# Query stage of a two-layer attention and expert kernel: sums of squares split between two engines, and the order of VectorE's steps

## The reference, cut to what matters

```python
x = x + _L0_xattn_ref(_layernorm(x, axis=-1), ctx_2048, ...)

# inside: 16 heads (NH) of 128 columns (HD)
q = (hidden_states @ Wq + bq).reshape(b, s, NH, HD)
var = jnp.mean(q * q, axis=-1, keepdims=True)      # one per token and head
q = q * jax.lax.rsqrt(var + 1e-6) * qn_w
```

## Time and profile before

| | us |
|---|---|
| median of 3 runs (4677.71 to 4683.45) | 4682.44 |
| the profiled execution: its own time | 4708.63 |
| the profiled execution: span of the profile | 4706.5 |
| of it the query stage | first 218 |

### The profile page before, as it was taken

How to read it: one execution, slowest core, us unless ns; L and a number is a source line. 1 busy time by engine, 2 the same in 40 slices (tenths; PEclk the granted TensorE clock), 3 DMA queues, 4 the chain that set the end, 5 groups by cost and what they waited for, 6 DMA issues and landing times. The chain is left out here.

```text
span 4706.5 us, 104529 instructions
## 1 busy us (share of the span) xinstructions
PE 3904.1 (83%) x34578; PEld 2973.1 (63%) x34579; DVE 3443.8 (73%) x5403; ACT 2449.9 (52%) x4087; POOL 2778.1 (59%) x2145
## 2 busy tenths in 40 slices
PE   5669999999999999999999735883199999999945
PEld 3437777767767776777777724773167767677734
DVE  4657787877877777878877236445789888888957
ACT  4635555545545555555555114331157777777843
POOL 5577777767767776777773144335635555555632
PEclk8879999999999999999999967996599999999966
DMA  6357777767767677687774547554344444444410
GB/s 242 113 133 148 167 153 160 168 132 162 161 141 163 145 159 150 152 173 150 155 160 103 172 127 215 140 141 126 113 123 130 119 123 125 124 118 129 110 38 25
DMA packets 1236097, 657.45 MB, mean 140 GB/s; under 512 B 1087825, under 2 KB 1162449, under 8 KB 1230654
## 3 DMA queue, kind: packets, MB, share of 16 engines
q1 hardware_dynamic: 1218654, 606.60, 54.8%
q0 software_dynamic: 9216, 22.03, 1.6%
q10 hardware_dynamic: 7760, 22.55, 1.3%
HBM read 187.16 MB, written 142.34 MB: 70 GB/s over the span
## 5 line engine op out<-in xcount | busy, mean ns | idle before, releaser
L2007 POOL TENSOR_TENSOR b_pTl<-b_pe,b_pTh 125x1344 f16<-125x1344 f32 x192 | 538.4, 2804 | 482.8 <-ACT b_pTh L2066 458.4
L111 PE MATMUL a_pa<-a_pTh,a_ch 125*128 125x224 f16 x3072 | 796.5, 259 | 1.9 <-DMA a_pTl<-a_pl 1.9
L113 PE MATMUL a_pa<-a_pTh,a_cl 125*128 125x224 f16 x3072 | 795.5, 259 | 0.0
L112 PE MATMUL a_pa<-a_pTl,a_ch 125*128 125x224 f16 x3072 | 795.4, 259 | 0.0
L826 POOL TENSOR_TENSOR a_ksq<-a_kb 125x512 f32<-125x512 f32 x384 | 474.0, 1234 | 350.9 <-DVE a_kb L759 283.4
L698 ACT ACTIVATE a_pr<-a_pr,a_nmax 112x1500 f32<-112x1500 f32 x256 | 395.7, 1546 | 374.3 <-DVE a_nmax L777 374.2
L843 POOL TENSOR_TENSOR a_kb<-a_kb,a_rk 125x512 f32<-125x512 f32 x384 | 540.4, 1407 | 69.1 <-POOL a_kb L843 34.8
L791 DVE SCALAR_TENSOR_TENSOR a_pl<-a_pr,a_inv,a_ph 112x1500 f16<-112x1500 f32 x256 | 502.3, 1962 | 46.1 <-ACT a_ph L705 45.2
L705 ACT ACTIVATE a_ph<-a_pr,a_inv 112x1500 f16<-112x1500 f32 x256 | 395.5, 1545 | 222.1 <-DVE a_inv L786 222.1
L2112 DVE TENSOR_REDUCE b_mx<-b_ps 112x3 f32<-112x1500 f32 x256 | 439.0, 1715 | 95.3 <-PE b_ps L2189 93.9
L777 DVE CUSTOM_DVE_ANT_0 a_pr<-a_ps,a_mask 112x1500 f32<-112x1500 f32 x256 | 438.8, 1714 | 70.3 <-PE a_ps L113 65.3
(11 more groups left out here) (376 smaller groups left out, 10953.5 us busy)
## 6 DMA issues: line engine op xcount, KB each, us to landing
b_ks<-b_kn SPq DMA_DIRECT2D x768, 93.8 KB
scratch_cT<-a_cT SPq DMA_DIRECT2D x64, 768.0 KB
b_cT<-scratch_cT SPq DMA_DIRECT2D x32, 1536.0 KB
a_ctx<-ctx SPq DMA_DIRECT2D x128, 360.0 KB
scratch_xd<-q_zero ACTq DMA_DIRECT2D x4, 4736.0 KB
scratch_yd<-e_y SPq DMA_DIRECT2D x74, 256.0 KB
scratch_oT<-a_ot SPq DMA_DIRECT2D x16, 896.0 KB, 4.2
m_oT<-scratch_oT SPq DMA_DIRECT2D x16, 896.0 KB
```

The source lines that it names most:

```text
L111: nc.tensor.matmul(out, a_hi, b_hi, start=start, stop=False)
L112: nc.tensor.matmul(out, a_hi, b_lo, start=False, stop=False)
L113: return nc.tensor.matmul(out, a_lo, b_hi, start=False, stop=stop)
L2007: nc.gpsimd.tensor_tensor(pTl[:, n % 2, :, 0:RP], pe_[:, n % NP], pTh[:, n % 2, :, 0:RP], ALU.subtract).then_inc(s["l_pool"], 1)
```

## The change

Three things change in `q0_phase`, and nothing elsewhere. ScalarE squares the first 11 heads of a tile only; VectorE squares and sums the other five, one operation per head, in a new step `square` placed between `split_x` and `split_q`, with a semaphore `q_sv` of its own that `sum_squares` also waits for. `shift(t+2)` becomes the first step of VectorE's turn. `variance` and GpSimd's `rstd` work for tile t+3 instead of t+2 in turn t, so both lists start one turn earlier, with turn -3.

```diff
+    ACT_HEADS = 11
...
-            pipeline(pool, NT, [(rstd, 2), (normalise, -1)])
+            pipeline(pool, NT, [(rstd, 3), (normalise, -1)])
...
-                for h in range(NH):
+                for h in range(ACT_HEADS):
...
+            def square(t, k, _):
+
+                dve.wait_ge(q_biased, 4 * t + 4)
+                for h in range(ACT_HEADS, NH):
+                    cols = slice(h * HD, (h + 1) * HD)
+                    nc.vector.tensor_tensor_reduce(out=qq[:, k, cols], in0=qb[:, k, cols], in1=qb[:, k, cols], scale=1.0,
+                                                   scalar=0.0, op0=ALU.mult, op1=ALU.add,
+                                                   accum_out=ss[:, k, h:h + 1]).then_inc(q_sv, 1)
+
             def sum_squares(t, k, _):
-                dve.wait_ge(q_sq, NH * t + NH)
+                dve.wait_ge(q_sq, ACT_HEADS * t + ACT_HEADS)
+                dve.wait_ge(q_sv, (NH - ACT_HEADS) * (t + 1))
                 nc.vector.tensor_scalar(ssv[:, k], ss[:, k], 1.0 / HD, RMS_EPS, ALU.mult, ALU.add).then_inc(q_ss, 1)
...
-            pipeline(dve, NT, [(variance, 2), (bias, 0), (sum_squares, -1), (shift, 2), (split_x, 1), (split_q, -2)])
+            pipeline(dve, NT, [(shift, 2), (variance, 3), (bias, 0), (sum_squares, -1), (split_x, 1), (square, 0),
+                               (split_q, -2)])
```

More of the change, by code:

```diff
@@ L202, in q0_phase @@
         out_done = [a.sem(f"q_out{i}") for i in range(2)]
-        w_hi = a.sem("q_w_hi")
+        w_hi, q_sv = a.sem("q_w_hi"), a.sem("q_sv")
         zeroed, empty = a.sem("q_zeroed"), a.sem("q_empty")
```

## The result

The changed kernel takes 4691.75 us in the median of 20 runs (4683.46 to 4699.95), the kernel before 4681.88 (20 runs beside it): a ratio of 1.0023, 95% interval 1.0016 to 1.0030, so 7.5 to 14.0 us slower. The forecast was +10.2.

What follows compares the result with a forecast made beforehand. Bounds: x landing beside the zero fill to 68 us, then two equal 9.68 us rings plus TensorE's slow clock. Terms 10.1 + 0.5 - 0.4 = +10.2 on 4682.44 gave 4692.6 us, range 4684.5 to 4702.5.

Steps and rivals of the forecast that it cites:

- The start: Query stage's first part: VectorE waits for x one tile further ahead, so each bias loses one landing, +10.1 us.
- Landings following issues: Rival: x of tile 5, issued 2 us later, lands 2 us later; 4694.6 us, chance 0.06.
- Shift first: VectorE's turn: nb issued at the turn's start removes 1.06 us between last bias and split_q, 2.27 to 1.21.
- Ring A: Loop of in-order VectorE with GpSimd, rq through qn, biases and sum back to rq; forecast to stay 9.68 us a turn.
- The rule on contention: Skill's rule: VectorE's two-SBUF-input operations contend with GpSimd reading SBUF; a square behind qn would cost up to 3.6 a turn.
- Ring B: Loop through TensorE: split_q, turn_q, project, turn_x, last bias, split_q; forecast to grow from 9.68 to 9.72 us.
- The squares are not dear: Denies the rival that the accumulator's read does not overlap, 0.37 us a square: +19.2, 4701.6 us, chance 0.18.
- Eleven heads on ACT: Last turn's wait for ACT's squares: 1.47 us less work but starting 1.10 later, -0.4 us.
- The term of the turns: Twelve turns of the query stage, each 0.04 us longer with the squares ahead of split_q, +0.5 us.
- with the clock's stretches unchanged: Condition on the +0.5 us: TensorE's stretches at 1.2 GHz instead of 2.4 stay as before in the twelve turns.

Runs made afterwards that it cites:

- Variance last: Changed kernel with variance(t+3) moved to the last place of VectorE's turn and GpSimd's rstd back to tile t+2; ratio 1.0008 to the kernel before.
- the small fill: Changed kernel with the same zero fill in sixteen quarter-sized transfers, four at the end of each of ScalarE's first four turns; ratio 0.9999 to the kernel before.
- one-input `nb`: Edit used in several runs: nb computed with one tensor input and rs as per-partition scalar; on the changed kernel, ratio 1.0015 to the kernel before.
- the third experiment: Changed kernel with only nb altered, to one tensor input and rs as per-partition scalar; ratio 1.0015 to the kernel before.
- the look-ahead kernels with one-input `nb`: Changed kernel with all sixteen heads squared on ScalarE and nb from one tensor input: ratio 0.9985 to the kernel before; with quarter-sized fill transfers too, 0.9968.
- squares only: Kernel before plus the five squares on VectorE alone, with its old step order and statistics two tiles ahead; ratio 1.0042 to the kernel before.
- the look-ahead kernel: Changed kernel with all sixteen heads squared on ScalarE, keeping shift first and statistics three tiles ahead; ratio 1.0006 to the kernel before.
- All together: Changed kernel with nb from one tensor input, quarter-sized fill transfers, sum_squares ahead of bias, squares behind split_q; 4662.16 us, ratio 0.9961; repeated, 4658.04 us, 0.9956.

## Why the prediction was right or wrong, point by point

**The start: right.** +10.1 was forecast; bias(0) is 10.10 later, tile 1 9.89, tile 2 9.75. Variance last takes the loss away without touching the fill; the small fill shortens it without touching the list. Landings following issues is refuted by tiles 4 and 5.

**Shift first: the mechanism right, its side effect missed.** The 1.06 us ahead of `xTl` went. But the prediction let `nb` be "issued at the turn's start" for nothing. That start lies under `qn`, `nb` has two tensor inputs in SBUF, and it waits for `qn` to end: 1.2 to 1.7 us longer in eleven turns, with `variance` and bias behind it. This is the step that failed, with "Ring A. Its sum stays 9.68": measured, `ssv` to `ssv` is 124.86 - 114.68 = 10.18 where Ring A binds, against 9.48 with one-input `nb`. In the turns between, where Ring B binds, part of it comes back (10.62 against 10.98), so at equal clock the wait is worth 0.17 a turn, some 2 us of the 3.84. The rule on contention was weighed, for the squares alone; the same rule held for the operation that the change moved.

**Ring B: too long.** 2.31 was forecast for the last bias to `split_q`, 2.04 measured, so it became shorter by 0.23 and not longer by 0.04: `xTl` to the next operation is 0.30, where I had kept the 0.52 of the earlier trace rows, which held a wait for `qTh`. The squares are 5 x 0.212 = 1.06 for 1.10. Ring A without `nb`'s wait is 9.48, not 9.68, as four biases take 2.41 when nothing holds them.

**The squares are not dear: right.** The accumulator's read overlaps, and the two inputs come at full rate: 0.21 a square. The Trainium skill, Vector Engine (DVE) Microarchitecture Reference, section "Points that are easy to get wrong", says that one form of instruction, `S2S2D2_STT`, has half the rate with two SBUF sources that are not bf16; whether these squares, a custom operation in the trace, have that form is not shown. 80 squares at a median of 289 ns don't show the halving.

**Eleven heads on ACT: the small term was wrong.** -0.4 forecast, +0.06 measured in the last turn. ACT's squares of the last tile start 4.35 behind the `ssv` in front of them (213.63 - 209.28) instead of 2.82 (198.51 - 195.69): 1.53 later, not 1.10, which takes back the 1.47 saved.

**The sum.** Forecast 10.1 + 0.5 - 0.4 = 10.2. The stage lost 9.75 + 3.84 + 0.06 = 13.65. The term of the turns was mis-sized, 3.8 instead of 0.5. The median moved by 9.9 us, and the interval (7.5 to 14.0) holds both. The 10 us of the start were worked out; that the total came within 0.3 us of the forecast, with the turns' term 3.3 us off in the profile, is luck.

**TensorE's clock: the condition did not hold.** The +0.5 stood "with the clock's stretches unchanged". They did not stay: 27.3 us of the twelve turns at 1.2 GHz instead of 17.1. Two turns alone, those from 124.86 to 148.13, are 2.5 us longer than the two before them; in the first of them the bias waits for TensorE three times, 1.6 us in all. The changed kernel with the small fill has three such pairs (12.11 to 12.19 and then 11.12), the third experiment and the look-ahead kernels with one-input `nb` have none; but squares only, in which `nb` never waits, has a stretch in every turn. So whether `nb`'s wait brings the clock down, or the squares do, or chance, is not shown, and what decides in which turn it falls was not tried: in the changed kernel the same stand of 1.98 us ahead of the second half of turn_q went with a fall in one turn (139.31) and not in another (116.97). A fall costs nothing where Ring B has room, as in the look-ahead kernel.

**Left open.** The mark and the medians do not agree to the last microsecond: the look-ahead kernel with one-input nb has the mark of the kernel before (220.92 and 221.00) and a ratio of 0.9985, whose interval excludes 1. All together ends the stage 12.4 us sooner, and its ratio of 0.9961 is 18.3 us (12.6 to 24.4); the changed kernel with the small fill ends it 5.5 us later at a ratio of 0.9999. What makes up the difference was not looked for.

## What to carry to other kernels

In a list that runs in order, a wait for a load that looks one tile further ahead holds everything written behind it; put the load's consumer last in the turn, or count a landing for each step of look-ahead. When an operation is moved, look at what another engine is doing at its new place, even if it has a single column. Before a few us of a loop are put down to an edit, compare turns at the same granted clock. An operation of VectorE that is issued under a long one of GpSimd should have one tensor input in SBUF.

## What the runs showed of the hardware

A one-column VectorE operation with two tensor inputs in SBUF took up to 2914 ns, ending within 0.02 us of GpSimd's 112x2048 multiply, and 205 ns with the same operands when one was a per-partition scalar. The Trainium skill, SBUF — State Buffer, section "Who interferes with whom", says that two SBUF inputs contend with a GpSimd instruction that reads SBUF; these runs agree for that multiply, and show it for an operation of one column. They do not agree for GpSimd's power of 112x16 numbers (2.9 us), which reads SBUF too: 74 of the changed kernel's 80 squares lie wholly under it, and none takes over 300 ns. By the trace's packets the 112 rows of a load of x pass in 8.7 us beside a fill in rows of 37.9 KB, which take 1.40 us each at the median, and in 2.2 to 4.0 us beside the same fill in rows of 9.5 KB, which take 0.36.
